# One core, attention with layer norm: token tiles kept by tokens and turned in the load of a block, their mean summed on GpSimd, queries of the preparing steps moved

## The reference

```python
xn = _layernorm(x, axis=-1)
# branch 1: causal linear attention, per head
q, k, v = elu(xn @ wq) + 1, elu(xn @ wk) + 1, xn @ wv
S_kv, z = running sums over tokens of k v^T and of k
o = (q S_kv) / (q z + EPS)
# branch 2: softmax attention over the batch's 2048 tokens
attn = softmax((q / |q| + query_embedding) * softplus(temperature) . k / sqrt(hd))
h = attn @ v;  out = h * masked_gates.sum(-1)      # top-3 gates and shared gates
return x + o @ wo + (out @ Wp.T + bp)
```

## Time and profile before

| | |
|---|---|
| three runs | 3873.67, 3873.71 and 3869.54 us, median 3873.67 |
| the profiled execution | 3873.82 us, of which the profile's span is 3870.4 |
| mean granted TensorE clock | 0.988 of full speed |
| instructions | 147623 |
| set-up, until the first projection | 0 to 98 us |
| preparing steps, until the first exponential | 98 to 240 us |
| steps 0 to 15 | 240 to 1103 us |
| steps 16 to 43 | 1103 to 2713 us |
| steps 44 to 63 and the end | 2713 to 3870 us |
| moved by DMA | 315.83 MB, mean 82 GB/s |

### The profile page before, as it was taken

The page is one execution under the profiler, slowest core; times in us unless marked ns, Lnnn a source line. Parts: engine busy times, 40 slices in busy tenths (PEclk is TensorE's granted clock), DMA queues, the critical chain, the costliest instruction groups (busy, mean ns, idle before and its releaser), DMA issues.

```text
span 3870.4 us, 147623 instructions
## 1 busy us (share of the span) xinstructions
PE 3708.2 (96%) x65983; PEld 1742.1 (45%) x65984; DVE 3362.6 (87%) x3595; ACT 2663.1 (69%) x2617; POOL 447.9 (12%) x229
## 2 busy tenths in 40 slices
PE   2889999999999999999999999999999999999999
PEld 1544444444444444444444444444444444444433
DVE  5668999899998989889898988889888888888986
ACT  3457777777777677677677677777767767767663
POOL 3101110011101101101110110100110110110120
PEclk8889999999999999999999999999999999999999
DMA  5322212222223313223222323313222221321323
GB/s 208 113 84 61 74 54 63 63 75 61 63 77 90 92 56 115 74 68 98 83 73 82 101 61 92 97 53 104 71 74 68 82 82 46 104 67 56 85 90 106
DMA packets 364210, 315.83 MB, mean 82 GB/s; under 512 B 158168, under 2 KB 312248, under 8 KB 362932
## 3 DMA queue, kind: packets, MB, share of 16 engines
q1 hardware_dynamic: 362852, 297.93, 25.8%
q10 hardware_dynamic: 720, 8.39, 0.5%
HBM read 230.74 MB, written 75.48 MB: 79 GB/s over the span
## 4 chain that ended last, share of the span: by engine, by line
PE 84%; ACT 7%; DVE 4%; issue 3%; SPq 1%; DMA 1%; POOL 0%; ACTq 0%; DVEq 0%; POOLq 0%
PE ps L1098 32%; PE ps L1263 22%; PE ps L1249 19%; ACT prob L924 6%; PE ps L1164 4%; PE ps L1193 2%; PE ps L1133 2%; PE ps L1187 1%; DVE acc L1815 1%; PE ps L1209 1%; SPq L446 1%; PE ps L1072 1%; PE ps L1230 0%; ACT r L868 0%; PE ps L1173 0%
## 5 line engine op out<-in xcount | busy, mean ns | idle before, releaser
L924 ACT ACTIVATE prob<-ps 128x2048 f32<-128x2048 f32 x1024 | 1924.4, 1879 | 604.9 <-PE ps L1249 601.9
L1815 DVE TENSOR_TENSOR acc<-acc,prob 128x2048 f32<-128x2048 f32 x896 | 2057.8, 2297 | 52.5 <-ACT prob L924 37.3
L1263 PE MATMUL ps<-prob,v 128*32 128x512 f32 x8192 | 1091.0, 605 | 0.0
L1249 PE MATMUL ps<-q_hi,k_hi 32*128 32x512 f16 x4096 | 420.0, 384 | 40.6 <-ACT prob L924 35.2
L1098 PE MATMUL ps<-x_hi,w_hi 128*32 128x512 f16 x4096 | 433.4, 383 | 0.4 <-DVE xt_lo L1599 0.4
L1098 PE MATMUL ps<-x_lo,w_hi 128*32 128x512 f16 x4096 | 433.1, 382 | 0.0
L1098 PE MATMUL ps<-x_hi,w_lo 128*32 128x512 f16 x4096 | 432.9, 382 | 0.0
L1249 PE MATMUL ps<-q_hi,k_lo 32*128 32x512 f16 x4096 | 409.9, 374 | 0.8 <-issue 0.8
L1249 PE MATMUL ps<-q_lo,k_hi 32*128 32x512 f16 x4096 | 409.2, 374 | 0.1
L1263 PEld LDWEIGHTS ps<-prob,v 128*32 128x32 f32 x8192 | 161.1, 108 | 433.2 <-issue 433.2
L1098 PE MATMUL ps<-wop_hi,fin 128*32 128x512 f16 x4096 | 348.8, 381 | 4.3 <-DMA y<-in_x 2.6
(11 more groups left out here) (263 smaller groups left out, 4381.6 us busy)
## 6 DMA issues: line engine op xcount, KB each, us to landing
x_hi<-xhi_scratch SPq DMA_DIRECT2D x64, 512.0 KB, 6.2
x_lo<-xlo_scratch SPq DMA_DIRECT2D x64, 512.0 KB, 7.4
x_in<-in_x SPq DMA_DIRECT2D x64, 256.0 KB, 7.1
rq<-rq_scratch SPq DMA_DIRECT2D x64, 256.0 KB
rdl<-rdl_scratch SPq DMA_DIRECT2D x64, 256.0 KB
y<-in_x SPq DMA_DIRECT2D x64, 256.0 KB, 5.9
out<-y SPq DMA_DIRECT2D x64, 256.0 KB, 5.8
rden<-rden_scratch SPq DMA_DIRECT2D x63, 256.0 KB
```

The source lines that it names most:

```text
L924: s_.activation(prob[i % 3][:], ps[:, 0:HG, :], ACT.Exp, bias=-SHIFT, scale=inv_c[:, g:g + 1] if wide else 1.0 / CQK).then_inc(exped, 2)
L1249: last = t_.matmul(bank[h], kk[rows32(h), cols128(kt)], qq[rows32(h), :], start=(kk is kh and qq is qh), stop=(kk is kl and not wide))
L1263: last = t_.matmul(bank[OUT][rows32(h), :], v[m // NB % 2][:, kt, rows32(h)], prob[i % 3][:, h, :], start=(kt == 0), stop=(kt == TT - 1))
L1815: v_.tensor_tensor(acc[:], acc[:], prob[i % 3][:], ALU.add).then_inc(summed, 1)
```

## The change

1. **Layout.** Tiles are normalised in place, and ScalarE and VectorE split them straight from x_in, by tokens (tokens on partitions). The scratch tensors hold rows of tokens. `turn_x` and its PSUM banks are gone. A block is turned as it is loaded: two transfers with `transpose=True`, each of 512 tokens by 512 values (L511 in the new file).
2. **Mean.** GpSimd adds up each tile (`sum_x`), the first of a batch being a copy. After a batch's last tile TensorE multiplies xsum with a column of 1/2048 (`mean_x`, four products into X0), and VectorE copies the result to fp16 (`keep_mean`); the following LK projection waits for that copy.
3. **Set-up.** All sixteen token tiles are issued ahead of the constants. The raw weights wait until the first eight tiles have landed. High and low halves of the first tiles lie in the buffers of x_hi, x_lo and fin, so that no tile waits for a store. The temperatures, norms, bounds and scales come at later rounds. The output weights' squares follow behind the tiles. Blocks 0 and 1 are both loaded in the set-up.
4. **Preparing steps.** The queries of block n + 1 are projected in slot 11 of step n, into bank 3, and ScalarE squares and copies them in slot 12. The second half of the values goes to bank 1 instead of waiting for X2. `turn_dl` moves behind `sum_q`, into bank 3. The splits of weights move from the start of their slots to the end.

```diff
-    xhi_d, xlo_d = scratch("xhi_scratch", [NT, P, KC * P]), scratch("xlo_scratch", [NT, P, KC * P])
+    xhi_d, xlo_d = scratch("xhi_scratch", [NT * P, D]), scratch("xlo_scratch", [NT * P, D])
...
-        x_hi, x_lo = ([sb(f"{n}{i}", [P, BT, KC, P], F16) for i in range(2)] for n in ("x_hi", "x_lo"))
+        x_hi, x_lo = ([sb(f"{n}{i}", [P, KC, BT * P], F16) for i in range(2)] for n in ("x_hi", "x_lo"))
+        def xn_of(t):
+
+            if t < 2 * BT:
+                return x_hi[t // BT][:, t % BT, :], x_lo[t // BT][:, t % BT, :]
+            if t < TT - 2:
+                return xn_first[t - 2 * BT][:, 0], xn_first[t - 2 * BT][:, 1]
+            return xn_hi[t % 2][:], xn_lo[t % 2][:]
...
+        def q_bank(n):
+            return bank[3] if n < NB else X1
+
+        def v_bank(n, i):
+            return bank[1] if i and n < NB else X2
+
+        def dl_bank(p):
+            return bank[3] if p < NB - 1 else X0
...
-        NORMS_AT, TEMPS_AT = 12, (4, 5, 7)
+        NORMS_AT, TEMPS_AT, SQUARES_AT, NORMS_OF = 16, (5, 8, 11), (5, 7, 9, 12), (9, 11, 13, 16)
...
-            load_first(0)
+            for i in range(TT // BT):
+                load_first(i)
...
-            for i in range(1, TT // BT):
-                load_first(i)
...
-                sp.wait_ge(x_turned, t - 1 if t >= TT + 2 else t - TT + 1)
+                sp.wait_ge(xlo_kept, t - 1 if t >= TT + 2 else t - TT + 1)
...
             def store_x(t):
+                stored = xf_stored[t // BT] if t < TT else xn_stored[t % 2]
                 sp.wait_ge(xhi_kept, t + 1)
-                sp.dma_start(xhi_d[t], xt_hi[t % 2][:].rearrange("p k n -> p (k n)")).then_inc(xt_stored[t % 2], 16)
+                sp.dma_start(xhi_d[t * P:(t + 1) * P], xn_of(t)[0]).then_inc(stored, 16)
                 sp.wait_ge(xlo_kept, t + 1)
-                sp.dma_start(xlo_d[t], xt_lo[t % 2][:].rearrange("p k n -> p (k n)")).then_inc(xt_stored[t % 2], 16)
+                sp.dma_start(xlo_d[t * P:(t + 1) * P], xn_of(t)[1]).then_inc(stored, 16)
             def load_block(n):
 
                 first = (n // (NB * NG) * NB + n % NB) * BT
-                for i in range(2):
-                    sp.wait_ge(xt_stored[i], (first + BT) // 2 * 32)
+                if n < NB * NG:
+                    sp.wait_ge(xf_stored[n % NB], BT * 32)
+                else:
+                    for i in range(2):
+                        sp.wait_ge(xn_stored[i], (first + BT - TT) // 2 * 32)
+                if n < 2:
+                    sp.wait_ge(x_summed, (n + 1) * BT)
                 if n >= 2:
                     sp.wait_ge(ql_proj, n - 1)
                 for tile, src in ((x_hi, xhi_d), (x_lo, xlo_d)):
-                    sp.dma_start(tile[n % 2][:].rearrange("p t k n -> p t (k n)"),
-                                 src[first:first + BT].rearrange("t p e -> p t e")).then_inc(xb_loaded[n % 2], 16)
+                    sp.dma_start(tile[n % 2][:], src[first * P:(first + BT) * P], transpose=True).then_inc(xb_loaded[n % 2], 16)
...
             for t in range(TT):
                 store_x(t)
-                if t == BT + 1:
-                    load_block(0)
+                if t in (BT + 1, 2 * BT + 1):
+                    load_block(t // BT - 1)
             load_x(TT)
...
             def sum_x(t):
                 pool.wait_ge(xhi_kept, t + 1)
                 pool.wait_ge(x_summed, t)
-                g_.tensor_tensor(xsum[:], xsum[:], xt_hi[t % 2][:].rearrange("p k n -> p (k n)"), ALU.add).then_inc(x_summed, 1)
+                if t % TT == 0:
+                    pool.wait_ge(xbar_mm, t // TT)
+                    g_.tensor_copy(xsum[:], xn_of(t)[0]).then_inc(x_summed, 1)
+                else:
+                    g_.tensor_tensor(xsum[:], xsum[:], xn_of(t)[0], ALU.add).then_inc(x_summed, 1)
...
+                if t is not None:
+                    sum_x(t)
...
+            act.wait_ge(x_first[1], BT * 16)
             for g in range(NG):
                 act.dma_start(w_raw[g][:], w6_d[g]).then_inc(wraw_in[g], 16)
...
-            def keep_x(t, bk):
-                act.wait_ge(x_turned, t + 1)
-                if t >= 2:
-                    act.wait_ge(xt_stored[t % 2], t // 2 * 32)
-                    act.wait_ge(x_summed, min(t - 1, TT))
-                s_.activation(xt_hi[t % 2][:].rearrange("p k n -> p (k n)"), bk, ACT.Copy).then_inc(xhi_kept, 1)
+            def keep_x(t):
+                act.wait_ge(ln_done, t + 1)
+                if t >= TT:
+                    act.wait_ge(xf_stored[-1], BT * 32)
+                    if t >= TT + 2:
+                        act.wait_ge(xn_stored[t % 2], (t - TT) // 2 * 32)
+                    act.wait_ge(x_summed, t - 1)
+                s_.activation(xn_of(t)[0], x_in[t if t < TT else t % 2][:], ACT.Copy).then_inc(xhi_kept, 1)
...
-                if t in (2, 4, 6, 8):
-                    square_w(t // 2 - 1)
-                if t in (10, 11):
-                    square_wop(t - 10)
-                if t == NORMS_AT + 1:
-                    act.wait_ge(scales_ready, 1)
-                    for a in range(6):
-                        split_w(0, a)
+                if t in SQUARES_AT:
+                    square_w(SQUARES_AT.index(t))
+            for i in range(2):
+                square_wop(i)
+            act.wait_ge(scales_ready, 1)
+            for a in range(6):
+                split_w(0, a)
...
+                    if kt == 12 and n is not None and n + 1 < NB:
+                        square_q(n + 1)
+                        keep_q(n + 1)
+                    if kt in SPLITS and split_group(s) is not None and s < 0:
+                        split_w(split_group(s), SPLITS.index(kt))
...
-            def turn_x(t, bk):
-                pe.wait_ge(ln_done, t + 1)
+            def mean_x(b):
+                pe.wait_ge(x_summed, (b + 1) * TT)
                 for k in range(KC):
-                    last = t_.transpose(bk[:, cols128(k)], x_in[t if t < TT else t % 2][:, cols128(k)], ident[:])
-                last.then_inc(x_turned, 1)
-            for t in range(TT):
-                if t >= 3:
-                    pe.wait_ge(xlo_kept, t - 2)
-                turn_x(t, (X0, X1, X2)[t % 3])
-                if t in (3, 5, 7, 9):
-                    norms(t // 2 - 1)
-                if t in (11, 12):
-                    norms_wop(t - 11)
-            pe.wait_ge(xlo_kept, TT)
+                    last = t_.matmul(X0[:, k:k + 1], xsum[:, cols128(k)], ones_s[:], start=True, stop=True)
+                last.then_inc(xbar_mm, 1)
+            for g in range(NG):
+                norms(g)
+            for i in range(2):
+                norms_wop(i)
+            mean_x(0)
...
-                    if kt == 0 and n is not None:
+                    if kt == 0 and n == 0:
+                        query(n)
+                    if kt == 0 and n is not None and n >= NB:
 
                         pe.wait_ge(dl_kept, n)
                         query(n)
                         if p is not None:
-                            pe.wait_ge(am_ready, 2 * p + 2)
-                            turn_dl(p)
+                            pe.wait_ge(am_ready, 2 * p + (2 if s >= 0 else 1))
+                            if s >= 0:
+                                turn_dl(p)
-                    if kt == 2 and p is not None:
+                    if kt == 2 and p is not None and s >= 0:
                         pe.wait_ge(rdl_kept, p + 1)
                     if kt == 2 and n is not None:
                         if mp is not None:
                             pe.wait_ge(den_kept, mp + 1)
                         sum_q(n)
+                        if p is not None and s < 0:
+                            turn_dl(p)
                         key(n)
-                        if t is not None:
-                            turn_x(t, X0)
-                        pe.wait_ge(v_kept, 2 * n + 1)
+                        if n >= NB:
+                            pe.wait_ge(v_kept, 2 * n + 1)
...
+                        if t is not None and t % TT == TT - 1:
+                            mean_x(t // TT)
+                            pe.wait_ge(xbar_ready, t // TT + 1)
                         project(X0, LK_, n, (0, 1))
...
+                    if kt == 11 and n is not None and n + 1 < NB:
+                        pe.wait_ge(qb_done, n + 1)
+                        pe.wait_ge(rdl_kept, n)
+                        query(n + 1)
...
-            def keep_x(t, bk):
+            def keep_x(t):
-                if t >= 2:
-                    dve.wait_ge(xt_stored[t % 2], t // 2 * 32)
-                v_.tensor_tensor(xt_lo[t % 2][:].rearrange("p k n -> p (k n)"), bk, xt_hi[t % 2][:].rearrange("p k n -> p (k n)"), ALU.subtract
-                                 ).then_inc(xlo_kept, 1)
-            def sum_x(t):
-                link(v_.tensor_reduce(xpart[:, :, t % TT], xt_hi[t % 2][:], AX.X, ALU.add))
-                if t % TT == TT - 1:
```

(16 more changed lines are left out.)

96 lines of the change are left out of this document (51 added, 45 removed).

## The result

| | before | changed |
|---|---|---|
| median of 5 runs, us | 3873.71 | 3888.7 |
| lowest to highest | 3869.54 to 3876.37 | 3883.27 to 3895.2 |
| ratio, 95% interval | | 1.0039 [1.0024, 1.0054] |
| profile's span | 3870.4 | 3886.3 |

The change makes the kernel slower by 0.4%, where 3838 was forecast. In the busy times of the page nothing looks wrong: TensorE works 32 us less than in the earlier trace rows, its share has fallen to 95%.

A forecast was written before the change was run, and what follows sets the result against it. TensorE was taken as the bound in the body, with VectorE the chain in late set-up. The sum -11 - 22 - 6 + 3 = -36 us from 3873.82 gave 3838 us, range 3814 to 3866 (8 in 10).

The forecast's parts named there:

- set-up: Ahead of the first projection, which would start at 87 instead of 98: minus 11 us.
- the preparing steps: Steps ahead of the first exponential: TensorE's waits covered and its clock kept up, minus 22 us.
- the body: Steps after the first exponential: minus 6 us for TensorE's transposes, plus 3 us for the means.
- the three means: Three times TensorE products and VectorE work precede a projection; a stall taken as 0.8 us, plus 3 us in all.
- the transposes: Four TensorE transposes leave slot 5: 0.21 us a step, in 28 steps, minus 6 us.
- The load itself: Turned transfers on SyncE's queue at the plain price; nothing moves if the pair takes some 9 or 10 us.
- rival 3: SyncE's queue: a slow turned load makes rden late; at three times plain +416, about 4290 us; chance 0.12.
- The second swallow: VectorE's idle time, 5.6 us a step, absorbs rden's lateness, so the pair decides only from about 16 us.
- The clock: Preparing steps: TensorE's clock stays up in three tails, 3.2 us each, 9.6 us of a possible 25.6.
- rival 1: Constants come late and VectorE takes over the preparing steps: set-up gains 6, preparing 8, about 3857 us; chance 0.22.
- The fourth step gains nothing: Last preparing step: no next query to pull in, so it gains nothing but its transpose.
- GpSimd: Sums of 48 tiles can stretch VectorE's accumulations, at worst 48 us, at best nothing; taken as zero.

The follow-up runs named there:

- The run at 12.5 us: Kernel before, its plain block load in slot 3 cut in fourteen transfers of 18 or 19 partitions: 4397.77 us, ratio 1.1353.
- the imitation: Kernel before, its plain block load in slot 3 cut in fourteen transfers of 16 or 32 partitions: 3894.36 us, ratio 1.0059.
- the run of part 3: Kernel before with part 4, plain load in slot 9, and part 3 with tiles still passing through PSUM: 3847.62 us, ratio 0.9935.

## Why the prediction was wrong

Against the forecast, set-up missed 3 us, the preparing steps 16 and the body 34.5. The body's 31.5 us are, by the slots in which they lie: 16.5 in slots 13 and 14 of steps 19, 23, 31, 35, 39 and 47, where the key-query product waits for y (forecast 0, the clock behind the waits included); 8.5 at the three means (forecast 3); 11.3 more of "issue" (forecast 0); and -5.9 for the transposes (forecast -6). That makes 30.4.

**The load itself: the step that failed.** The price of landing was right in size, 8.0 and 5.1 us against 6.2 and 7.4. The term that was missed is the issue, 7.9 us of SyncE in place of 1. I said that up to some 9 or 10 us for the pair nothing would move, and that rival 3 would decide from 16. The pair was inside that bound (8.0 us of issue, 10.2 until it had landed, by the medians of the pairs), and the kernel lost all the same: the room was read wrong. It was taken as the 9.0 us from x_hi's issue to that of rden's way back. But rden's way out stands 2 us ahead of the way back, and the queue has other issues in between. Step 43 of the kernel before:

```profile
2670.03 1.55 SPq L511 DMA_DIRECT2D hlo_scratch<-h_lo  x1
2674.72 0.32 SPq L573 DMA_DIRECT2D rden_scratch<-rden_c  x1
```

Only 2674.72 - 2671.58 = 3.1 us are free. So a pair that takes more than 1.0 + 3.1 = 4.1 us makes rden late there, and with the margin of 2.3 us at VectorE (2686.14 less 2676.75 and a landing of 7.1) one of over 6.4 us makes VectorE late. The second swallow that I added, VectorE's idle time as a mean over all steps, 5.6 us each, isn't there in every fourth step, in which the loss falls: in steps 19, 23, ..., 43 of the kernel before it is 1.9 to 2.8 us. Step 43, which I called typical, is one of these. The queue's place and the victim were named as in rival 3 (it had 0.12); its size, +416 us, was that of three times the plain price. The run at 12.5 us shows that such sizes do come, at less than I set. That the turned pair costs its queue time is shown by the imitation and by the same waits in the changed kernel's trace, not by a run that takes the turned load alone away.

By the Trainium skill (VectorE: DVE Perf Modes, The three transpose paths) the estimate was 42 us for a pair if its squares ran one after another; the trace shows 8.0 and 5.1 to landing, 13 us even if the two medians are laid end to end, so the squares don't run one after another. By the Trainium skill (DMA: Bandwidth & Descriptors, Latency and other measured facts) the estimate was 4 us for the pair; the rows have more than that for either half. Neither figure says anything of the issuing queue, and most of the cost arose there.

**TensorE's stalls.** I counted nothing for the block load's effect on TensorE. "issue" went from 10.7 to 25.6 us in the changed kernel (4.0 of it in the preparing steps) and to 2.4 with a plain load in slot 9. Runs show that the load's place makes them. The traces also show what they are. The queue that brings TensorE's instructions moved 16 KB at a time:

```profile
q8 instruction: 521, 8.54, 0.9%
```

That is one packet per 255 of TensorE's instructions. Every one of the 16 stalls in the body of the kernel before, and of the 21 of the changed one, ends 1.2 to 1.6 us after such a packet has landed. In all 37 that packet started 2.2 to 8.1 us after the issue of the block load; of the body's other packets about one in eight did. And it came late: TensorE had begun 290 to 535 instructions since the packet before it started, where the median is 251 to 254. So TensorE stands because its next instructions are late. That the block's transfers hold them up on the DMA engines fits this and is not shown, nor is why packets behind a load in slot 9 are not held up.

**Set-up: right, -8.1 for -11.** The first projection at 89.9, forecast 87. The constants were in VectorE's hands at 39.06, forecast 37. That the gain is from leaving out the ping-pong over PSUM agrees with the run of part 3, which can't tell it from the buffers.

**Preparing steps: half right in mechanism, wrong in sum, -5.8 for -22.** The three tails' waits for phkT, phqT and sq are gone as forecast, turning the denominators waits 1.37, 1.52 and 1.52 for the 1.5 forecast, but two terms fell short. The clock, by stretch from the first projection to the first exponential, before and after:

```profile
97.98:239.41 141.43, 112.80 (x2335) 77.62 (x2339) 82.84 (x189) 55.15 (x106) 14.81 (x8) 0.83 0.35 115
```

```profile
89.86:225.47 135.61, 105.44 (x2319) 73.25 (x2323) 83.00 (x186) 55.11 (x106) 19.64 (x12) 0.85 0.44 113
```

The lower level cost 0.17 x 141.4 = 24.0 us and now 0.15 x 135.6 = 20.3: some 4 came back (the clock is rounded) where 9.6 was forecast. The clock still falls behind waits, which are now others. And the claim failed that little would be late next. TensorE's waits in the stage, without the one ahead of its first product, sum to 30.2 us, where they were 28.5: new are two for the keys' maximum (1.43 and 1.49), one for k_lo (1.70), two without a releaser (2.23 and 1.73), and the last tail, 8.83 where it was 4.42, for rq:

```profile
206.71 0.43 SPq L599 DMA_DIRECT2D rq_scratch<-rq_c  x1
210.45 0.56 SPq L602 DMA_DIRECT2D rq<-rq_scratch  x1
...
216.26 0.69 DVE L1761 TENSOR_TENSOR qb<-qb,rq 128x512 f32<-128x512 f32 x1 [7.48 <-DMA rq<-rq_scratch]
217.61 2.08 PE L1201 MATMUL ps<-phqT,phkT 32*128 32x128 f32 x16 [8.83 <-DVE phqT L1798]
```

The sign that was given for rival 1, a stage of over 130 us with VectorE as releaser, was there: 135.6 us, and VectorE released 20 of the 30.2. Yet VectorE is busy for only 83.0 us of the stage; the longest of these waits goes back to rq, that is to SyncE's queue.

"The fourth step gains nothing" was the sentence that should have been a question: it loses 5.2 us from its key-values product to the first exponential.

**The transposes: right.** Slot 5 of a step with a token tile is now 1582.78 - 1579.80 = 2.98 us, as against the 3.19 of the earlier trace rows:

```profile
1579.80 1.88 ACT L962 ACTIVATE prob<-ps 128x2048 f32<-128x2048 f32 x1 [0.19 <-PE ps L1286]
1582.78 1.88 ACT L962 ACTIVATE prob<-ps 128x2048 f32<-128x2048 f32 x1 [0.58 <-PE ps L1286]
```

(step 24). The 6 us were won and can't be seen in the total.

**The mean: mis-sized.** Forecast +3 for three places, measured 1.6 + 2.7 + 4.1 = 8.5, all in slot 7 or 8 of steps 11, 27 and 43. The waits themselves were 0.5, 1.6 and 1.6 us, inside the bound of 2.3 and half as much again as the 0.8 taken. The four products were put at 0.2 us, like the transposes; in step 43 they hold TensorE for 1.05 (the row of L1113 above), and in the other two places what is left beside the wait is 1.1. And in step 43 the lower clock behind the wait costs 1.7.

**GpSimd: right that it costs nothing by itself, too low in its worst case.** 61.5 us of stretching in the changed kernel against the 48 given as the worst; the sums alone made 41, without effect. Most of both lies beside y's addition, alone or with a sum. That addition now stands behind the sum in GpSimd's order, which was not counted.

## What to carry to other kernels

Price a transfer three ways: bytes, landing, and the time that its issue holds the queue; the last is what others behind it pay, and it need not follow from the bytes. Count what else the queue has to issue in between. Read the margin of what stands behind it in the step that is fullest, not in a typical one or as a mean, since a periodic step without idle time makes a small delay into a steep loss. Then look for the place in the queue where nobody waits: moving one plain load by six slots was worth more here than the whole change was meant to win in the body.
